# A graph layer on one core: the second level of v in two halves, and the order around it, in the first group

## What is computed

```python
h1 = relu(bn1(conv1(h)))                     # 1x1 convolution over the features
x_conv = relu(bn2(conv2(h1)) + h)            # 17 taps along the nodes
s = h @ w_se.T + b_se                        # 3 numbers for each node
A = exp(-dist(s)) * adj
msg = relu(h @ w_msg.T + b_msg)
x_nmp = A @ msg
gi = concat(x_conv, x_nmp) @ w_ih.T + b_ih   # a GRU cell: gates r, z, n
gh = h @ w_hh.T + b_hh
out = x + (1 - z) * n + z * h
```

## Time and profile before

| what | value |
|---|---|
| median of 3 runs | 281.13 us (280.69 to 281.86) |
| the profiled execution's own time | 280.81 us |
| its span, first to last instruction | 279.0 us |
| granted TensorE clock, mean | 0.999 |
| TensorE busy (matmul) | 271.0 us, 97% |
| VectorE busy | 243.9 us, 87% |
| ScalarE busy | 163.7 us, 59% |
| GpSimd busy | 65.8 us, 24% |

### The profile page before, as it was taken

One profiled execution on the slowest core, in us unless ns is written; L12 is line 12 of the kernel. 1 busy time (PEld: TensorE's weight loads), 2 busy tenths in 40 slices (PEclk: granted clock), 3 DMA queues, 4 the chain that ended last, 5 costly groups with the idle time before them and its releaser, 6 DMA issues.

```text
span 279.0 us, 5223 instructions
## 1 busy us (share of the span) xinstructions
PE 271.0 (97%) x1800; PEld 244.9 (88%) x1800; DVE 243.9 (87%) x550; ACT 163.7 (59%) x275; POOL 65.8 (24%) x127
## 2 busy tenths in 40 slices
PE   7899999999999999999999999999999999999993
PEld 6599877999889988899889998899889998899883
DVE  6999979998999889987999989988999887984666
ACT  3797468737753677517754567527674276541563
POOL 7900021820225002610206102430026100340000
PEclk9999999999999999999999999999999999999999
DMA  6940405655234544172642634364440604053002
GB/s 236 354 64 0 153 1 185 236 88 172 79 152 61 131 158 154 78 100 100 225 153 40 111 136 157 136 89 112 150 153 8 104 16 150 2 62 60 2 0 75
DMA packets 20797, 31.00 MB, mean 111 GB/s; under 512 B 9778, under 2 KB 14644, under 8 KB 19892
## 3 DMA queue, kind: packets, MB, share of 16 engines
q1 hardware_dynamic: 17552, 26.47, 28.9%
q0 software_dynamic: 3072, 4.20, 11.2%
q10 hardware_dynamic: 148, 0.01, 0.0%
HBM read 25.64 MB, written 8.70 MB: 123 GB/s over the span
## 4 chain that ended last, share of the span: by engine, by line
PE 82%; DVE 11%; ACT 3%; POOL 1%; issue 1%; DMA 1%; DVEq 0%
PE ps L1329 24%; PE ps L1331 24%; PE ps L1330 23%; PE ps L1397 5%; PE ps L1440 4%; DVE wt_lo L887 2%; DVE stats L845 1%; POOL rstd L419 1%; PE ps L1418 1%; DMA xin<-x_first 1%; ACT wt_hi L500 1%; DVE mv L902 0%; DVE v_lo L968 0%; DVE y L999 0%; DVE n_lo L1049 0%
## 5 line engine op out<-in xcount | busy, mean ns | idle before, releaser
L1331 PE MATMUL ps<-v_hi,wt_lo 128*128 128x256 f32 x280 | 78.8, 281 | 0.0
L1329 PE MATMUL ps<-v_hi,wt_hi 128*128 128x256 f32 x280 | 78.7, 281 | 0.0
L1330 PE MATMUL ps<-v_lo,wt_hi 128*128 128x256 f32 x280 | 78.6, 281 | 0.0
L1329 PEld LDWEIGHTS ps<-v_hi,wt_hi 128*128 128x128 f32 x280 | 52.7, 188 | 0.6
L1330 PEld LDWEIGHTS ps<-v_lo,wt_hi 128*128 128x128 f32 x280 | 52.7, 188 | 0.5
L1331 PEld LDWEIGHTS ps<-v_hi,wt_lo 128*128 128x128 f32 x280 | 52.6, 188 | 0.0
L425 POOL TENSOR_TENSOR scale<-vpe,neg_half 128x8 f32<-128x8 f32 x6 | 10.6, 1768 | 84.8 <-DVE scale L862 84.8
L594 ACT ACTIVATE mbs<-ps,par 128x256 f32<-128x256 f32 x24 | 12.1, 505 | 29.7 <-DVE y L988 17.6
L1329 PE MATMUL ps<-h_hi,wt_hi 128*128 128x512 f32 (+1 forms) x65 | 25.8, 396 | 0.3 <-DVE h_lo L897 0.3
L1331 PE MATMUL ps<-h_hi,wt_lo 128*128 128x512 f32 (+1 forms) x65 | 25.0, 384 | 0.0
L1330 PE MATMUL ps<-h_lo,wt_hi 128*128 128x512 f32 (+1 forms) x65 | 24.9, 384 | 0.0
(11 more groups left out here) (177 smaller groups left out, 636.5 us busy)
## 6 DMA issues: line engine op xcount, KB each, us to landing
w<-ln_rows SPq DMA_DIRECT2D x6, 1024.0 KB, 4.6
mask<-adj_t SPq DMA_DIRECT2D x8, 512.0 KB, 3.5
out<-x_t SPq DMA_DIRECT2D x7, 512.0 KB, 5.4
out<-gate POOLq DMA_DIRECT2D x14, 256.0 KB, 4.2
xin<-x_nm SPq DMA_DIRECT2D x6, 512.0 KB, 4.5
xt<-x_t SPq DMA_DIRECT2D x6, 512.0 KB, 4.3
slot_rows<-turned SPq DMA_DIRECT2D x24, 32.0 KB, 3.1
rows<-slot_rows SPq DMA_DIRECT2D x6, 128.0 KB, 2.5
```

The lines of the kernel that those rows point to most:

```text
L1329: pe.matmul(dst, wt_hi[:, blk, :], hi, start=start, stop=False)
L1330: pe.matmul(dst, wt_hi[:, blk, :], lo, start=False, stop=False)
L1331: return pe.matmul(dst, wt_lo[:, blk, :], hi, start=False, stop=stop)
```

## The change

Only the first group's order changes. The second level's two differences are each made, rounded and split by themselves. VectorE: level2_b(0, 0), lot 2, the low half 0, lot 3, level2_b(0, 1), the low half 1. ScalarE: lots 2 and 3, the high half 0, a copy of h, lot 4, the other copy of h, the high half 1. On VectorE level2_u(0) moves ahead of join_b(0, 0) and lot 6. On ScalarE v_high_u(0, 1) moves ahead of lots 8, 9 and 10. TensorE waits for the first halves on two new semaphores.

```diff
+        v_hib_half, v_lob_half = sem("v_hib_half"), sem("v_lob_half")
...
-            def hf_rows_first():
-                for c, src in ((0, 6), (1, 7)):
-
-                    act.wait_ge(h_lo_ready, c + 1)
-                    act.activation(hf[0][:, cols(c)], bank(src), ACT.Relu).then_inc(hf_ready, 1)
+            def hf_rows_first(c, src):
+
+                act.wait_ge(h_lo_ready, c + 1)
+                act.activation(hf[0][:, cols(c)], bank(src), ACT.Relu).then_inc(hf_ready, 1)
...
+            def v_high_b_first(i):
+                act.wait_ge(vtb_ready, i + 1)
+                act.activation(v_hi[:, 1 + i, 1:1 + VN, :], vtb[:, i],
+                               ACT.Copy).then_inc(v_hib_ready if i else v_hib_half, 1)
...
             lot_high(2)
+            lot_high(3)
             act.wait_ge(pads_set, 6)
-            hf_rows_first()
-            lot_high(3)
-            v_high_b(0, 1)
+            v_high_b_first(0)
+            hf_rows_first(0, 6)
             lot_high(4)
+            hf_rows_first(1, 7)
+            v_high_b_first(1)
             act.wait_ge(row_split, 3)
             by_graphs(0, 0, 6)
             by_graphs(0, 1, 7)
             lot_high(5)
             v_high_u(0, 0)
             m_shared(0, 0)
-            for n in range(6, 11):
+            lot_high(6)
+            lot_high(7)
+            v_high_u(0, 1)
+            for n in range(8, 11):
                 lot_high(n)
-            v_high_u(0, 1)
             messages(0, 3)
...
+            def v_low_b_first(i):
+                dve.wait_ge(v_hib_ready if i else v_hib_half, i + 1)
+                dve.tensor_tensor(v_lo[:, 1 + i, 1:1 + VN, :], vtb[:, i], v_hi[:, 1 + i, 1:1 + VN, :],
+                                  ALU.subtract).then_inc(v_lob_ready if i else v_lob_half, 1)
...
             level2_b(0, 0)
+            lot_low(2)
+            v_low_b_first(0)
+            lot_low(3)
             level2_b(0, 1)
-            lot_low(2)
-            lot_low(3)
-            v_low_b(0, 1)
+            v_low_b_first(1)
             lot_low(4)
             level1(0)
             lot_low(5)
             v_low_u(0, 0)
+            level2_u(0)
             join_b(0, 0)
             lot_low(6)
-            level2_u(0)
             lot_low(7)
             v_low_u(0, 1)
             join_b(0, 1)
...
                 if i == 0:
-                    pe.wait_ge(v_hib_ready, 1 + min(v, 1))
+                    if v == 1:
+                        pe.wait_ge(v_hib_half, 1)
+                    else:
+                        pe.wait_ge(v_hib_ready, 1 + v // 2)
...
                 if i == 0:
-                    pe.wait_ge(v_lob_ready, 1 + min(v, 1))
+                    if v == 1:
+                        pe.wait_ge(v_lob_half, 1)
+                    else:
+                        pe.wait_ge(v_lob_ready, 1 + v // 2)
```

## The result

| | before | after |
|---|---|---|
| median of 16 runs each | 280.72 us (280.52 to 281.86) | 281.90 us (281.73 to 282.99) |
| ratio to before, 95% interval | | 1.0031 (1.0020 to 1.0043) |
| span of the profiled execution | 279.0 us | 280.3 us |
| first gate product of n starts | 34.87 us | 36.10 us |

The change makes the kernel slower, by 1.18 us between the medians, by 0.31% (0.9 us) in the ratio that is taken round by round.

What follows compares the result with a forecast made beforehand. The prediction took VectorE's full in-order queue before n_low to set the start of TensorE's gates of n, and TensorE's pace the rest. +0.63 - 0.19 + 0.77 - 0.06 = +1.15 us gave a 282.3 us median, range 281.1 to 283.0.

Steps and rivals of the forecast that it cites:

- The bound: Group 0 up to n_low: VectorE's full queue sets when TensorE starts the gates of n, 34.87 us before the change.
- The first hole: VectorE before v_low_b_first(1): idle 0.56 us waiting for ScalarE's second high half; lot_low(4) at 16.13, +0.63 with the split.
- The split: VectorE, level2_b made as two halves instead of one operation: costs 0.06 us.
- v_low_u(0, 1): VectorE's low half of u: starts at 22.25 instead of 21.81, +0.44, as its earlier 0.20 wait for ScalarE is gone.
- The messages: ScalarE's messages start at 23.42, 1.20 later, behind lots 8 to 10; VectorE's slot steps wait, adding 0.77.
- TensorE: Gains 0.3 us near 14.10, gives it back at sub-convolution 4 (23.01); gathers 0.92 late cost nothing; gates of n at 36.02.
- The size: Whole kernel: +1.15 us, +0.41%, stated as a median of 282.3 us.
- The four terms of the sum: VectorE up to n_low: +0.63 halves, -0.19 net at v_low_u(0, 1), +0.77 slots, -0.06 at masked.
- One hole only: Slot stage doesn't pay the full 0.77, ScalarE catching up or VectorE's steps shorter: about +0.6, 281.7 us; chance 20%.
- no net change: Delays eaten by group 1's waits and TensorE's free 0.43 before n_lo: about +0.1, 281.2 us; chance 7%.
- Faster: No VectorE hole at 15.3, n_low before 33.53, TensorE's 0.3 from 14.1 kept: 280.8 us; chance 8%.
- Worse than my sum: Delays add: n_high or join_y late gives VectorE a further hole up to 0.5: +1.65, 282.8 us; chance 15%.

Runs made afterwards that it cites:

- the two pads: Kernel before plus one 512-column VectorE operation: 281.40 us against 280.75, ratio 1.0016; kernel before plus two TensorE products on zeros: 281.13 against 280.75, ratio 1.0004.
- the run with the hole filled: Changed kernel with VectorE's lot_low(3) put between level2_b(0, 1) and its low half: 281.76 us against 280.81 for the kernel before, ratio 1.0028.
- the kernel with the trip covered: Changed kernel: VectorE's lot_low(3) behind level2_b(0, 1), ScalarE's second high half ahead of h's second copy, lots 8 to 10 ahead of v_high_u(0, 1): 281.10 us, ratio 1.0010.
- The two kernels with a lot on GpSimd: Low part of lot 12 moved from VectorE to GpSimd: on the kernel before 281.15 us, ratio 1.0021; on the changed kernel 282.19, ratio 1.0053.

## Why the prediction was right

- **The bound.** VectorE's queue up to n_low, not TensorE, sets the start of the gates: shown by the two pads, +0.61 for a VectorE operation, +0.03 for TensorE's 0.47 us.
- **The first hole.** Forecast 0.56 and lot 4 at 16.13; measured 0.58 start to start and 16.24 (16.18 without the start's own 0.06). The reason given, "nothing stands between them", holds for this kernel by a hair: vtb was ready at 15.40 and ScalarE free at 15.37, where the prediction had 15.30 and 15.23. Both ends were in its numbers, but it named only VectorE's. That ScalarE's copy of h would hold the second high half nearly as long once VectorE's side is covered it didn't say, and the expectation of the run with the hole filled failed on just that.
- **The split.** Forecast 0.06. Start to start the halves take 0.35 each (14.02 to 14.37) against 0.62 for both at once, so 0.08; over the whole stretch from vtb to lot 4, less the hole, it is 0.09 (3.20 - 0.58 against 2.53), and 0.12 in the kernel with the trip covered. The formula of the Trainium skill's page "VectorE: DVE Perf Modes", section on the TRN2 errata, would give 0.16, an estimate. The traces lie below it.
- **v_low_u(0, 1).** Forecast 22.25, measured 22.35.
- **The messages.** Forecast 23.42, measured 23.52; ssq at 23.70, measured 23.78; the lot behind at 25.27, measured 25.35. The whole detour through ScalarE's three lots is shown by undoing it (-0.55) and by doing it alone (+1.48).
- **TensorE.** Forecast the third phase near 14.10, the wait in sub-convolution 4 until 23.01, the gates of n at 36.02. Measured 14.15, 23.11 and 36.10. The gathers were 1.08 late (31.64 against 30.56) and not 0.92, still inside VectorE's 1.23, and so without effect. The wait is shown as 0.66, where I wrote "near 0.8"; counted from 22.18, when TensorE was due, it is about 0.9, and the 0.66 is what the profile leaves idle after the modelled ends.
- **The size.** Forecast +1.15, or +0.41%. In the trace 1.17, between the medians 1.18; the ratio gives 0.31% (0.20 to 0.43). The point 282.3 was 0.4 above the measured median of 281.9, since it stood on the median of the three runs shown, 281.13, and of 16 runs it is 280.72; with that the same sum gives 281.87. The four terms of the sum, +0.63, -0.19, +0.77 and -0.06, came out at +0.68, -0.20, +0.75 and -0.06 with the start's own 0.06 taken off, so the total isn't right by luck.
- **The rivals.** "One hole only" and "no net change" are out: both holes stand in the trace, and nothing in group 1 gave a part back (the wait for h_lo is still 0.3). "Faster" is out: n_low started at 34.76 and not before 33.53, and TensorE's 0.3 was lost at sub-convolution 4. "Worse than my sum" is out as well: n_high was done at 34.23, before n_low could start.

## What to carry to other kernels

In a stage where several engines work in order for each other, ask of each not how busy it is but whether anything is free on it before the point that the next stage waits for; a moved instruction costs there by what it leaves behind itself. When a step goes to another engine and back, both queues have to be looked at: covering work on the sender does nothing while the receiver is at something else. And an instruction that waits shouldn't be put ahead of work that could run now, unless what it releases is on the bound: here three lots behind one early wait cost 1.48 us alone.

## What was not expected of the hardware

A GpSimd tensor_tensor on SBUF held up VectorE's operation with two SBUF inputs for 1.26 us (1.94 against 0.68), though not the one with an input in PSUM (0.48 as ever). In the changed kernel, where GpSimd's operation began at 28.00 beside such a PSUM join, it took 1.83; where it began at 27.52 during a VectorE lot that ran to 28.02, it took 2.21, so the hold seems to go both ways. No run has GpSimd's operation alone, so this isn't shown.

Single traces of the same group of steps differ elsewhere by more than the effect in question: the kernel with level2_u moved alone has its gate of n at the same 34.87 as before and yet a span of 279.7 us. Its list of waits has one that the kernel before doesn't show:

```profile
PE ps L1418 <- DMA rows<-slot_rows: 0.7, 1, 0.7
```

It is a wait of the distances in a later group, between 170 and 200 us, for the rows' DMA. The two kernels with a lot on GpSimd have the same wait in their traces, of 0.6 and 0.4 us, in the same stretch. These three are the traces whose execution took 0.6 to 0.9 us longer than the median of its kernel (281.55 against 280.66, 281.90 against 281.15, 282.80 against 282.19). None of the other traces has the wait, and none of their executions is more than 0.23 above its median. That this wait is what makes some executions of every kernel longer is likely but not shown, as only one execution of each has a trace. So a span alone can't rank two kernels here that are 0.7 us apart; the position of the step in question, beside the medians, can.
